# A kernel of two chained per-batch products: the result stores move from SyncE's queue to ScalarE's

## The chip, the cores and the metric

The kernel runs on one core of one Trainium2 chip. The metric is the device time of one execution in microseconds. Names of engines: PE is TensorE, DVE is VectorE, ACT is ScalarE, POOL is GpSimd, SP is SyncE, whose only work is to issue transfers and wait for them.

## The reference, cut to what matters

```
# x (128, 64, 512); itok_B_0_7, itok_B_1_198 (128,); weights (8, 64, 64) and (200, 64, 64)
w = L0_cond_weights[itok_B_0_7];   x = x + einsum('bct,bcd->bdt', x, w)
w = L1_cond_weights[itok_B_1_198]; x = x + einsum('bct,bcd->bdt', x, w)
```

Each of the 128 batches is a matrix of 64 channels by 512 time steps. It is multiplied by one of 8 matrices and added to itself, then the same with one of 200 matrices. x and the result are 16.8 MB each, in fp32.

## The kernel before

**What is computed.** For each batch the two steps are one 64x64 matrix, (W0 + 1)(W1 + 1). The kernel builds these matrices on the chip and multiplies each batch once.

**Tiles.** Four batches make a slot: 128 partitions by 1024 numbers, 0.5 MB. There are 32 slots (0 to 31), and two of them make a unit of 1 MB; there are 16 units (0 to 15). All of x stays in one SBUF tensor, `xy`, with a place of its own for each slot. The results are written over x there, and are stored from there. So no load waits for room, and no store frees any.

**The start.** SP loads the indices, unit 0 and slot 2. ACT loads the 8 first matrices and the other indices. POOL gathers the second matrices, one for each batch (2.1 MB, an indirect transfer on a queue of its own). PE turns the matrices (L175, L190; L180 is repeated work that keeps PE busy meanwhile), and DVE and ACT copy them (L248, L298). SP issues slot 3 and units 2 to 15 (L121) once DVE has copied the first 16 of the first matrices.

**The loop.** The 16 units are grouped in blocks: unit 0, unit 1, and then two units each (`BLOCKS`). `products` (L210) multiplies the two matrices of each batch of a block into PSUM. `copy_m` (L262) on DVE and ACT brings them to `m_diag`. `apply` (L229) multiplies the slots of a block, 8 matmuls for each slot as the trace counts them, into two of six PSUM banks, so three slots are in flight (`Y_RING` is 3): slot s waits for the copies of slot s - 3 on both engines. `copy_y` (L270) copies a slot's result from PSUM to `xy`; DVE takes one half of the batches' channels and ACT the other, two copies each for every slot.

**Order.** Nothing here is placed by a scheduler. PE's order is products(0), then for each block k products(k + 1) and apply(k). DVE and ACT run the same function `copies`: for each block the copies of its slots, then `copy_m` of block k + 2 (whose waits are L254 and L257). SP issues all loads and then all stores, on one queue. A store of unit v waits for both engines' copies of the unit's second slot; the last unit is stored as two slots:

```
            for v in range(UNITS - 1):
                store(2 * v, 2)
            store(SLOTS - 2, 1)
            store(SLOTS - 1, 1)
            for v in range(UNITS):
                sp.wait_ge(s_out[v], 32 if v == UNITS - 1 else 16)
```

`s_y_v` and `s_y_s` count the copies done on DVE and on ACT, two for each slot, and `s_out` the stores that have landed. `s_y_psum` counts the slots that PE has finished.

Of the kernel before, what the change touches and what calls it, by code (L numbers as in the profile page):

```python
# [5 lines left out]
def bass_cond_residual_kernel(  # L6
# [31 lines left out]
    SLOTS = B // SLOT  # L38
    UNIT = 2 * SLOT
    UNITS = B // UNIT  # L40
# [25 lines left out]
    out_view = out_dram.rearrange("(s b) (q i) t -> (b q) s (i t)", b=SLOT, i=J)  # L66

    ctx = ExitStack()
    with ctx:  # L69
        def sb(name, shape, dt):  # L70
            return ctx.enter_context(nc.sbuf_tensor(name, shape, dt))

        def sem(name):
            return ctx.enter_context(nc.semaphore(name))

        xy = sb("xy", [P, SLOTS, J * T], fp32)
# [34 lines left out]
        s_y_v = sem("s_y_v")  # L111
        s_y_s = sem("s_y_s")
        s_x = [sem(f"s_x{n}") for n in range(UNITS)]
        s_out = [sem(f"s_out{n}") for n in range(UNITS)]
# [3 lines left out]
        @block.sync  # L118
        def _(sp):
            def load(s, n):  # L120
                sp.dma_start(xy[:, s:s + n, :], x_view[:, s:s + n, :]).then_inc(s_x[s // 2], 16)  # L121

            sp.dma_start(cond[:, :], cond_dram.rearrange("(b o) -> b o", o=1)).then_inc(s_cond, 16)
            load(0, 2)
            load(2, 1)

            sp.wait_ge(s_w0b_early, EARLY * UNIT)
            load(3, 1)
            for v in range(2, UNITS):
                load(2 * v, 2)  # L130
            def store(s, n):

                sp.wait_ge(s_y_v, 2 * (s + n))
                sp.wait_ge(s_y_s, 2 * (s + n))
                sp.dma_start(out_view[:, s:s + n, :], xy[:, s:s + n, :]).then_inc(s_out[s // 2], 16)

            for v in range(UNITS - 1):
                store(2 * v, 2)
            store(SLOTS - 2, 1)
            store(SLOTS - 1, 1)  # L140
            for v in range(UNITS):
                sp.wait_ge(s_out[v], 32 if v == UNITS - 1 else 16)

        @block.gpsimd
        def _(pool):
            nc.gpsimd.memset(ident[:, :], 0.0).then_inc(s_zeros, 1)
            pool.wait_ge(s_zeros, 1)
            nc.gpsimd.affine_select(out=ident[:, :], in_=ident[:, :], compare_op=ALU.not_equal, fill=1.0,
                                    base=0, pattern=[[-1, P]], channel_multiplier=1).then_inc(s_ident, 1)

            pool.wait_ge(s_cond, 16)
            nc.gpsimd.indirect_dma_start(
                out=w1_rows[:, :, :].rearrange("b d e -> b (d e)"), out_offset=None,
                in_=w1_dram.rearrange("s d e -> s (d e)"),
                in_offset=bass.IndirectOffsetOnAxis(ap=cond[:, 0:1], axis=0)).then_inc(s_gather, 16)

            pool.wait_ge(s_subjects, 16)
            for first in range(EARLY * UNIT, B, 2 * UNIT):
                _, picked = nc.values_load_multi_w_load_instructions(  # L159
                    subjects[0:1, first:first + 2 * UNIT], engines=(POOL,), min_val=0, max_val=S0 - 1,  # L160
                    skip_runtime_bounds_check_because="subjects index the 8 matrices")
                if first == EARLY * UNIT:
                    pool.wait_ge(s_gather, 16)
                    pool.wait_ge(s_w0t, 4)
                for n in range(2 * UNIT):
                    v, odd, r = (first + n) // UNIT, n // SLOT % 2, n % SLOT
                    nc.gpsimd.tensor_copy(w0b[HALVES[odd], v * SLOT + r, :],  # L167
                                          w0t[HALVES[odd], bass.ds(picked[n] * C, C)]).then_inc(s_w0b, 1)
# [74 lines left out]
        def copy_w1(eng, copy, done, n):  # L243

            eng.wait_ge(s_w1_turned, n + 1)
            turned = psum[0:C, n % W1_RING, :].rearrange("q (k v o r) -> q o v r k", k=TURN, o=2, r=SLOT)
            for odd, rows in enumerate(HALVES):
                copy(w1[rows, :, n * TURN:(n + 1) * TURN].rearrange("q (v r) k -> q v r k", r=SLOT),  # L248
                     turned[:, odd, :, :, :]).then_inc(done, 1)

        def copy_m(eng, scale, done, odd, k):

            first, n = BLOCKS[k]
            eng.wait_ge(s_m_psum, k + 1)  # L254
            if first + n > M_RING:

                eng.wait_ge(s_y_psum, 2 * (first + n - M_RING))  # L257
            at = first % M_COLUMNS * J * C
            to = m_diag[:, odd, first % M_RING:first % M_RING + n, :, :].rearrange(
                "q v j (i b e) -> q b (v j) i e", i=J, b=2)  # L260
            for b in range(2):
                scale(to[:, b, :, :, :],  # L262
                      psum[:, M_BANKS[k] + odd, at:at + n * J * C].rearrange("q (w e i) -> q w i e", i=J, e=Q),
                      mask[:, b:b + 1]).then_inc(done, 1)

        def copy_y(eng, copy, done, i, s):

            eng.wait_ge(s_y_psum, s + 1)
            for h, rows in enumerate(HALVES):
                copy(xy[rows, s, i * T:(i + 1) * T], psum[HALVES[i], 2 * (s % Y_RING) + h, :]).then_inc(done, 1)  # L270

        def copies(eng, copy, scale, w1_done, m_done, y_done, odd):
            for n in range(odd, TURNS, 2):
                copy_w1(eng, copy, w1_done, n)
            eng.wait_ge(s_mask, 2 * SLOT)
            copy_m(eng, scale, m_done, odd, 0)
            copy_m(eng, scale, m_done, odd, 1)
            for k, (first, n) in enumerate(BLOCKS):
                for s in range(2 * first, 2 * (first + n)):
                    copy_y(eng, copy, y_done, odd, s)  # L280
                if k + 2 < len(BLOCKS):
                    copy_m(eng, scale, m_done, odd, k + 2)

        @block.vector
        def _(dve):
# [10 lines left out]
            for rows in HALVES:  # L296
                for j in range(J):
# [3 lines left out]
                        one[:, j, :, :, :].to_broadcast((C, S0, Q // J, J)), ALU.add).then_inc(s_w0t, 1)  # L301

            _, picked = nc.values_load_multi_w_load_instructions(
                subjects[0:1, 0:EARLY * UNIT], engines=(DVE,), min_val=0, max_val=S0 - 1,
                skip_runtime_bounds_check_because="subjects index the 8 matrices")
# [7 lines left out]
            diagonal = w1_rows[:, :, :].rearrange("b d e -> b (d e)")[:, ::C + 1]  # L313
            nc.vector.tensor_scalar_add(diagonal, diagonal, 1.0).then_inc(s_w1_plus, 1)  # L314
            copies(dve, nc.vector.tensor_copy, nc.vector.tensor_scalar_mul, s_w1_v, s_m_v, s_y_v, 0)

        @block.scalar
        def _(act):
            act.dma_start(w0_rows[:, :, :], w0_dram.rearrange("s (k j) d -> (s k) j d", j=ROWS)  # L319
                          ).then_inc(s_w0_rows, 16)  # L320
            act.dma_start(subjects[:, :], subject_dram.rearrange("(o b) -> o b", o=1)).then_inc(s_subjects, 16)

            act.wait_ge(s_w0_rows, 16)
            for n in range(TICKS):
                if n >= 1:
                    act.wait_ge(s_tick, n)
                nc.scalar.copy(w1[:, 0:ROWS, :], w0_rows[:, :, :]).then_inc(s_tick, 1)  # L327
            copies(act, nc.scalar.copy, nc.scalar.mul, s_w1_s, s_m_s, s_y_s, 1)


# [24 lines left out]
```

## Time and profile before

| | |
|---|---|
| median of 3 runs | 92.88 us (92.86 to 92.94) |
| the profiled execution | 92.97 us |
| its span, first to last instruction | 91.2 us |
| mean granted PE clock in the span | 0.976 |
| bytes moved | 35.93 MB, of them 16.8 MB loads of x and 16.8 MB stores |

The span is what the profile covers; 1.8 us of the profiled execution lie around it. A share of busy time is a share of the span. "Landing" of a transfer is the time from its issue until all of it has arrived and its semaphore says so. SP's waits and the time that an issue takes aren't counted as busy work. A queue is named by the profile: q1 is SP's, q10 is ACT's, q0 is POOL's.

### The profile page before, as it was taken

To read this page: it belongs to the slowest core of one execution; us is meant where nothing else is said; L and a number is where in the kernel's file an instruction comes from. 1 tells how busy PE (TensorE), PEld (TensorE's weight loads), DVE (VectorE), ACT (ScalarE), POOL (GpSimd) and SP (SyncE) were. 2 spreads that over 40 slices of the span, in tenths; PEclk is the share of its full clock that TensorE was granted. 3 is DMA by queue.
4 is the path that set the end of the run, shared out by engine and by line. 5 is a ranking of instruction groups with operands and counts; after the bars stand their busy time and mean duration, and the time that the engine had idled before them with its cause. 6 is when DMAs were issued, how large, how long until landed. Compare 5 with 4: busy or idle time off the path is not lost.

```text
span 91.2 us, 2427 instructions
## 1 busy us (share of the span) xinstructions
PE 79.2 (87%) x890; PEld 45.6 (50%) x890; DVE 61.8 (68%) x127; ACT 58.6 (64%) x117; POOL 23.4 (26%) x119
## 2 busy tenths in 40 slices
PE   0599979985999999999999999999999999999100
PEld 0488959974454544454454445445545444443000
DVE  1096009996287878787888787888778888788600
ACT  2899806886276776676777576777657676676500
POOL 3400039989999988000000000000000000000000
PEclk9999999999999999999999999999999999999955
DMA  0999999999999999999999999999999999999992
GB/s 12 335 438 422 453 361 420 411 406 415 406 408 408 406 408 413 415 394 417 408 403 415 420 419 420 410 424 415 419 415 419 415 422 422 419 419 404 417 404 104
DMA packets 9181, 35.93 MB, mean 394 GB/s; under 512 B 721, under 2 KB 850, under 8 KB 9042
## 3 DMA queue, kind: packets, MB, share of 16 engines
q1 hardware_dynamic: 8880, 33.56, 91.5%
q0 software_dynamic: 144, 2.10, 5.4%
q8 instruction: 7, 0.11, 0.5%
q10 hardware_dynamic: 146, 0.13, 0.5%
q14 instruction: 4, 0.03, 0.1%
HBM read 19.01 MB, written 16.78 MB: 392 GB/s over the span
## 4 chain that ended last, share of the span: by engine, by line
PE 70%; DMA 12%; DVE 9%; issue 1%; DVEq 1%; ACTq 0%; POOLq 0%
PE psum L229 62%; DMA w_rows<-in_L_cond_weights_dram,cond 10%; DVE w L248 7%; PE psum L210 7%; DMA subjects<-in_itok_B_dram 2%; DVEq L69 1%; DVE xy L270 1%; PE psum L190 1%; DVE m_diag L262 1%; ACTq L319 0%; DVE w_rows L314 0%; POOLq L159 0%; DVEq L254 0%
## 5 line engine op out<-in xcount | busy, mean ns | idle before, releaser
L229 PE MATMUL psum<-xy,m_diag 64*128 64x512 f32 x256 | 57.1, 595 | 0.5 <-DVE m_diag L262 0.5
L270 DVE COPY xy<-psum 64x512 f32<-64x512 f32 x64 | 43.7, 684 | 13.1 <-PE psum L229 12.1
L270 ACT COPY xy<-psum 64x512 f32<-64x512 f32 x64 | 37.2, 581 | 19.8 <-PE psum L229 19.0
L229 PEld LDWEIGHTS psum<-xy,m_diag 64*128 64x128 f32 x256 | 25.2, 187 | 26.7 <-issue 25.4
L167 POOL COPY w0b<-w0t 64x64 f32 x112 | 21.6, 235 | 10.1 <-DMA w_rows<-in_L_cond_weights_dram,cond 8.4
L210 PEld LDWEIGHTS psum<-w,w0b 64*32 64x32 f32 x512 | 5.6, 105 | 6.4 <-issue 3.8
L248 ACT COPY w<-psum 64x256 f32<-64x256 f32 x16 | 5.8, 364 | 4.0 <-PE psum L190 3.0
L180 PE MATMUL psum<-ident,w_rows 128*64 128x128 f32 x54 | 8.1, 326 | 0.0
L262 DVE TENSOR_SCALAR m_diag<-psum,mask 128x256 f32<-128x256 f32 (+1 forms) x18 | 7.2, 448 | 1.1 <-PE psum L210 0.9
L190 PE MATMUL psum<-ident,w_rows 128*64 128x128 f32 x64 | 7.2, 274 | 0.7 <-DVE w_rows L314 0.7
L327 ACT COPY w<-w_rows 128x256 f32<-128x256 f32 x18 | 7.3, 404 | 0.8 <-DMA w_rows<-in_L_cond_weights_dram 0.2
L180 PEld LDWEIGHTS psum<-ident,w_rows 128*64 128x64 f32 x54 | 7.3, 137 | 0.7
L210 PE MATMUL psum<-w,w0b 64*32 64x64 f32 x512 | 6.9, 224 | 0.9 <-DVE w L248 0.9
L262 ACT ACTIVATE m_diag<-psum,mask 128x256 f32<-128x256 f32 (+1 forms) x18 | 7.0, 447 | 0.9 <-PE psum L210 0.7
L248 DVE COPY w<-psum 64x256 f32<-64x256 f32 x16 | 6.7, 418 | 1.2 <-PE psum L190 0.8
L190 PEld LDWEIGHTS psum<-ident,w_rows 128*64 128x64 f32 x64 | 7.0, 151 | 0.9 <-DVE w_rows L314 0.9
L175 PE MATMUL psum<-ident,w_rows 128*64 128x128 f32 x4 | 1.0, 414 | 3.4 <-DMA w_rows<-in_L_cond_weights_dram 3.4
L298 DVE TENSOR_TENSOR w0t<-psum,ident 64x256 f32<-64x256 f32 x4 | 1.5, 412 | 3.3 <-PE psum L175 3.3
L314 DVE TENSOR_SCALAR w_rows<-w_rows 128x64 f32<-128x64 f32 x1 | 0.2, 224 | 4.2 <-DMA w_rows<-in_L_cond_weights_dram,cond 4.2
L327 ACT ACT_TABLE_LOAD x1 | 1.3, 1283 | 1.8 <-issue 1.8
L309 DVE COPY w0b<-w0t 64x64 f32 x16 | 2.1, 187 | 0.2
L175 PEld LDWEIGHTS psum<-ident,w_rows 128*64 128x64 f32 x4 | 0.5, 159 | 3.4 <-issue 3.4
(8 smaller groups left out, 2.3 us busy)
## 6 DMA issues: line engine op xcount, KB each, us to landing
xy<-in_x_dram SPq DMA_DIRECT2D x15, 1024.0 KB, 18.5
out_dram<-xy SPq DMA_DIRECT2D x15, 1024.0 KB, 14.8
xy<-in_x_dram SPq DMA_DIRECT2D x2, 512.0 KB, 5.9
out_dram<-xy SPq DMA_DIRECT2D x2, 512.0 KB, 4.7
w_rows<-in_L_cond_weights_dram ACTq DMA_DIRECT2D x1, 128.0 KB, 2.5
cond<-in_itok_B_dram SPq DMA_DIRECT2D x1, 0.5 KB, 2.3
subjects<-in_itok_B_dram ACTq DMA_DIRECT2D x1, 0.5 KB
w_rows<-in_L_cond_weights_dram,cond POOLq DMA_INDIRECT x1, 9.3
```

Of the source, the lines that this page charges most:

```text
L167: nc.gpsimd.tensor_copy(w0b[HALVES[odd], v * SLOT + r, :], w0t[HALVES[odd], bass.ds(picked[n] * C, C)]).then_inc(s_w0b, 1)
L175: last = nc.tensor.transpose(w0_psum[:, z * P:(z + 1) * P], w0_rows[:, z, :], ident[:, :])
L180: nc.tensor.transpose(psum[0:C, z, 0:P], w0_rows[:, z, :], ident[:, :])
L190: last = nc.tensor.transpose(psum[0:C, n % W1_RING, z * B:(z + 1) * B], w1_rows[:, :, n * TURN + z], ident[:, :])
L210: last = nc.tensor.matmul(psum[QUARTERS[r], M_BANKS[k] + odd, at:at + C], w0b[rows, v * SLOT + r, j * Q:(j + 1) * Q], w1[rows, v * SLOT + ...
L229: last = nc.tensor.matmul(psum[:, 2 * (s % Y_RING) + h, :], m_diag[rows, odd, v % M_RING, j, :], xy[rows, s, j * T:(j + 1) * T], start=j = ...
L248: copy(w1[rows, :, n * TURN:(n + 1) * TURN].rearrange("q (v r) k -> q v r k", r=SLOT), turned[:, odd, :, :, :]).then_inc(done, 1)
L262: scale(to[:, b, :, :, :], psum[:, M_BANKS[k] + odd, at:at + n * J * C].rearrange("q (w e i) -> q w i e", i=J, e=Q), mask[:, b:b + 1]).the ...
L270: copy(xy[rows, s, i * T:(i + 1) * T], psum[HALVES[i], 2 * (s % Y_RING) + h, :]).then_inc(done, 1)
L298: nc.vector.tensor_tensor(w0t[rows, :].rearrange("q (s j k y) -> q j s k y", s=S0, j=J, y=J)[:, j, :, :, :], turned[:, j, :, :, :], one[:, ...
L309: nc.vector.tensor_copy(w0b[HALVES[odd], v * SLOT + r, :], w0t[HALVES[odd], bass.ds(picked[n] * C, C)]).then_inc(s_w0b_early, 1)
L327: nc.scalar.copy(w1[:, 0:ROWS, :], w0_rows[:, :, :]).then_inc(s_tick, 1)
```

## The change

The stores leave SP. `store` becomes a function in the outer scope that issues on ACT's own queue, with the same two waits, now executed by ACT. In `copies`, ACT alone (`odd` is 1 there) calls it after the copies of each even slot s above 0, for the unit that ended with slot s - 1. The two stores of the last unit stand at the end of ACT's program. SP issues the loads and then waits for all stores, as before.

```
--- before
+++ after
@@ block.sync
             for v in range(2, UNITS):
                 load(2 * v, 2)
-            def store(s, n):
-
-                sp.wait_ge(s_y_v, 2 * (s + n))
-                sp.wait_ge(s_y_s, 2 * (s + n))
-                sp.dma_start(out_view[:, s:s + n, :], xy[:, s:s + n, :]).then_inc(s_out[s // 2], 16)
-
-            for v in range(UNITS - 1):
-                store(2 * v, 2)
-            store(SLOTS - 2, 1)
-            store(SLOTS - 1, 1)
             for v in range(UNITS):
                 sp.wait_ge(s_out[v], 32 if v == UNITS - 1 else 16)
@@ after copy_y
+        def store(s, n):
+
+            nc.scalar.wait_ge(s_y_v, 2 * (s + n))
+            nc.scalar.wait_ge(s_y_s, 2 * (s + n))
+            nc.scalar.dma_start(out_view[:, s:s + n, :], xy[:, s:s + n, :]).then_inc(s_out[s // 2], 16)
+
@@ copies
                 for s in range(2 * first, 2 * (first + n)):
                     copy_y(eng, copy, y_done, odd, s)
+                    if odd and s % 2 == 0 and s > 0:
+
+                        store(s - 2, 2)
@@ block.scalar
             copies(act, nc.scalar.copy, nc.scalar.mul, s_w1_s, s_m_s, s_y_s, 1)
+            store(SLOTS - 2, 1)
+            store(SLOTS - 1, 1)
```

The last rows of ACT's program before, slots 28 to 31. A row is an instruction with its line, and in brackets the semaphores that it waits for:

```order
L270 COPY xy<-psum 64x512 [waits s_y_psum]
L270 COPY xy<-psum 64x512
L270 COPY xy<-psum 64x512 [waits s_y_psum]
L270 COPY xy<-psum 64x512
L270 COPY xy<-psum 64x512 [waits s_y_psum]
L270 COPY xy<-psum 64x512
L270 COPY xy<-psum 64x512 [waits s_y_psum]
L270 COPY xy<-psum 64x512
L69 UNCONDITIONAL_BRANCH
```

And of the change, the same four slots (its line numbers are smaller by 10; L260 is L270 of before, L266 is the store):

```order
L260 COPY xy<-psum 64x512 [waits s_y_psum]
L260 COPY xy<-psum 64x512
L266 DMA out_dram<-xy 128x2x1024 [waits s_y_s,s_y_v]
L260 COPY xy<-psum 64x512 [waits s_y_psum]
L260 COPY xy<-psum 64x512
L260 COPY xy<-psum 64x512 [waits s_y_psum]
L260 COPY xy<-psum 64x512
L266 DMA out_dram<-xy 128x2x1024 [waits s_y_s,s_y_v]
L260 COPY xy<-psum 64x512 [waits s_y_psum]
L260 COPY xy<-psum 64x512
L266 DMA out_dram<-xy 128x1024 [waits s_y_s,s_y_v] x2
L69 UNCONDITIONAL_BRANCH
```

The stores of units 13 and 14 stand behind the copies of slots 28 and 30, and those of slots 30 and 31 behind all copies.

SP's program before, whose rows are the loads and then the stores:

```order
L123 DMA cond<-in_itok_B_1_198_dram 128x1
L121 DMA xy<-in_x_dram 128x2x1024
L121 DMA xy<-in_x_dram 128x1024
L121 DMA xy<-in_x_dram 128x1024 [waits s_w0b_early]
L121 DMA xy<-in_x_dram 128x2x1024 x14
L135 DMA out_0_dram<-xy 128x2x1024 [waits s_y_s,s_y_v] x15
L135 DMA out_0_dram<-xy 128x1024 [waits s_y_s,s_y_v] x2
```

In the changed kernel the two rows of L135 are gone from SP, and the five above them stay as they are. The order on PE, DVE and POOL is the same in both kernels.

## Rows read from the trace of the kernel before

**Rows 1.** The page's part 2: busy tenths in 40 slices of the span
```profile
PE   0599979985999999999999999999999999999100
...
DMA  0999999999999999999999999999999999999992
```

**Rows 2.** The chain that ended last: start us, us, what; from 22.44 us on
```profile
22.44 3.70 PE psum L229 x16
...
39.21 7.07 PE psum L229 x32
...
70.70 13.96 PE psum L229 x64
84.66 0.02 issue
84.68 0.68 DVE xy L270
85.36 0.72 DVEq L69
```

**Rows 3.** Busy time by stretch, with PEclk, DMA share and GB/s at the end
```profile
7.00:14.00 7.00, 6.35 (x51) 5.87 (x50) 1.95 (x14) 3.81 (x10) 1.09 (x6) 1.00 0.97 402
28.00:35.00 7.00, 7.00 (x94) 3.32 (x94) 5.47 (x10) 4.56 (x9) 6.45 (x35) 1.00 1.02 405
35.00:42.00 7.00, 7.00 (x94) 3.32 (x94) 5.77 (x10) 5.12 (x10) 1.10 (x6) 1.00 1.03 409
49.00:56.00 7.00, 7.00 (x94) 3.38 (x94) 5.86 (x9) 5.25 (x10) 0.00 (x0) 1.00 1.03 420
77.00:84.00 7.00, 7.00 (x34) 3.10 (x32) 5.60 (x9) 4.78 (x9) 0.00 (x0) 1.00 1.02 416
84.00:91.00 7.00, 0.63 (x4) 0.00 (x0) 1.73 (x3) 1.31 (x3) 0.00 (x0) 0.71 0.79 321
```

**Rows 4.** DMA queues of the whole span: packets, MB, share of 16 engines
```profile
q1 hardware_dynamic: 8880, 33.56, 91.5%
```

**Rows 5.** SP's last load issue (L121, duration in ns, landing in us), and its first store
```profile
L121 SPq DMA_DIRECT2D xy<-in_x_dram x1: 5425/5425/5425, 29.7 to 29.7; - x1
...
DMA to landing us min/median/max: 21.0/21.0/21.0
...
35.20 2.27 SPq L135 DMA_DIRECT2D out_dram<-xy  x1
```

**Rows 6.** Timeline of ACT: its copies of slot 2 and of slot 5
```profile
28.90 0.58 ACT L270 COPY xy<-psum 64x512 f32<-64x512 f32 x1 [0.67 <-PE psum L229]
...
35.04 1.19 ACT L270 COPY xy<-psum 64x512 f32<-64x512 f32 x2 [0.53 <-PE psum L229]
```

**Rows 7.** The last three stores (L135), and the timeline from 82 us on
```profile
L135 SPq DMA_DIRECT2D out_dram<-xy x3: 345/345/372, 82.7 to 86.1; - x3
...
DMA to landing us min/median/max: 4.6/4.7/5.6
...
82.67 3.78 SPq L135 DMA_DIRECT2D out_dram<-xy  x3
...
82.97 1.19 ACT L270 COPY xy<-psum 64x512 f32<-64x512 f32 x2 [0.53 <-PE psum L229]
...
84.68 1.40 DVE L270 COPY xy<-psum 64x512 f32<-64x512 f32 x2 [0.32 <-PE psum L229]
```

**Rows 8.** The first issues of ACT and SP, and the landing of ACT's first
```profile
0.75 0.41 ACTq L319 DMA_DIRECT2D w_rows<-in_L_cond_weights_dram  x1
1.18 0.54 ACTq L321 DMA_DIRECT2D subjects<-in_itok_B_dram  x1
...
0.75 0.38 SPq L123 DMA_DIRECT2D cond<-in_itok_B_dram  x1
...
w_rows<-in_L_cond_weights_dram ACTq DMA_DIRECT2D x1, 128.0 KB, 2.5
```

**Rows 9.** The wait of L257 near 46.3 us, and ACT's timeline there
```profile
L257 ACTq EVENT_SEMAPHORE  x1: 17/17/17, 46.3 to 46.3; - x1
...
46.33 1.19 ACT L270 COPY xy<-psum 64x512 f32<-64x512 f32 x2 [0.53 <-PE psum L229]
```

**Rows 10.** ACT's longest wait: us in total, times, longest
```profile
ACT xy L270 <- PE psum L229: 19.0, 32, 1.6
```

**Rows 11.** DMA queues from 10 to 12 us, the gather (q0) beside the loads
```profile
q0 software_dynamic: 49, 0.56, 65.4%
q1 hardware_dynamic: 31, 0.13, 17.8%
```

## The prediction

> **What bounds the kernel now.** I read four views in this order: busy shares, the chain of waits, the transfers by stretch, the single stores at the end.
>
> The page's head [rows 1] shows two resources full at once: PE at 9 tenths nearly everywhere, and the 16 DMA engines at 9 in 38 of 40 slices, moving some 410 GB/s. The chain of waits [rows 2] runs from 22.44 us on through PE alone (32 slots, with short pieces of L210 between) to 84.66 us, then through DVE's last two copies. So PE sets when the last result exists. But the DMA engines are not waiting for it: in the stretches [rows 3] they move 405 to 409 GB/s while only loads are in flight (28 to 49 us), 416 to 420 while only stores are (56 to 84 us), and 321 on average in the last stretch, where the work runs out. All 33.56 MB of x and result lie on SP's one queue, q1, in issue order [rows 4]: the last load is issued at 29.7 us and lands 21.0 us later, at 50.7; the first store therefore moves nothing before 50.7, though SP issues it at 35.2 [rows 5] and slot 2, the one after its own two, is already copied from 28.9 on [rows 6].
>
> Is the end set by PE or by the queue? Two stores answer [rows 7]. The 1 MB store of unit 14 takes 5.6 us from issue to landing, the 0.5 MB store of slot 31 4.6 us. Unloaded, 128 KB took 2.5 us [rows 8], of which 0.13 MB / 410 GB/s = 0.3 is transfer: 2.2 us fixed (estimate, from a load). The two would then need 2.2 + 2.6 = 4.8 and 2.2 + 1.3 = 3.5 us. So 0.8 to 1.1 us of each is queueing behind older bytes. The bound at the end is the **transfer total**, with PE only about 1 us behind it.
>
> **The change, part by part.**
>
> *Bytes and instructions.* The same 17 stores of the same shapes; 17 issues leave SP and go to ACT. No copy, matmul or load is changed. The only thing that can move the end is when stores reach the DMA engines and how fast these work with two queues in flight.
>
> *ACT's time.* 17 issues x 0.372 us (the issue of an unblocked store [rows 7]; ACT's own took 0.406 and 0.542 [rows 8]) = 6.3 to 9.2 us on ACT's sequencer. Does it delay copies? The wait of L257 stands behind the two copies of a slot in ACT's program, and it is recorded at 46.3 us, when the copies have just begun (46.33 to 47.52) [rows 9]. So the sequencer runs ahead of the engine, and an issue runs beside the copies in front of it. A slot lasts 1.72 us (82.97 to 84.68 [rows 7]), its two copies 1.19: 0.54 us at most, begun with the copies, ends before they do. ACT also waited 19.0 us for PE in 32 waits [rows 10]. Cost: 0.
>
> *The added waits.* The stores' waits now stand in ACT's stream, and the copies of the next slot are queued behind them. For unit v they ask for both engines' copies of slot 2v+1, and they are reached when slot 2v+2 is done on PE. DVE's two copies take 1.40 us [rows 7], less than a slot of 1.72, so the wait is already met. Only the last two stores are different: nothing is queued behind them. Cost: 0.
>
> *How late the stores come.* Unit 14: SP issued it at 82.67, now it follows slot 30's copies, whose release is at 82.97: 0.3 us later (not 1.7, since the sequencer runs ahead). Slot 30: from 84.4 to about 84.7, after slot 31's copies are dispatched. Slot 31: waits for DVE's copy, which ends at 86.08, as before. The queueing of 0.8 us on unit 14 covers the 0.3. Cost: 0; without that cover it would be 0.3.
>
> *How early they come.* Store 0 can go at 28.9 us, when slot 2's copies begin [rows 6], and need not wait behind the loads of its queue until 50.7. From about 30 us both kinds share the engines. Loads that have not landed at 30: 20.7 us x 0.407 = 8.4 MB, units 8 to 15. At half of 412 GB/s, 206, they last until 70.8 us. PE starts unit 15 at 82.97 - 1.72 = 81.2. So loads stay 10 us ahead, PE keeps its pace, and the bytes are only reordered. Work is conserved: gain 0.
>
> Is half right? The nearest row with two queues in flight is the gather beside the loads: from 10 to 12 us 49 packets on q0 and 31 on q1 [rows 11], so neither queue starves the other. The loads need 8.4 MB in 51 us, 164 GB/s, 40% of 412.
>
> *Rate with both directions mixed.* Nothing in this trace shows it: loads and stores never overlap. The bounds are the nearest stretches: all at 405 or all at 420 [rows 3] over the 41 us of mixing. At 405 instead of 412, 41 x 1.7% = 0.7 us later; at 420, 0.8 us earlier. Below 405 lies only the 402 of the stretch with gather and loads on two queues, and it also holds SP's wait. I take 412, the middle: it is what the same bytes get now. The early end is capped: 2.1 MB remain to be issued from 83.0 on, so the last landing is at 83.0 + 2.2 + 5.1 = 90.3 against 90.7 now (86.1 + 4.6), 0.4 us; and since the 2.2 is an estimate from a load, I let the range go to 0.7.
>
> [...]
>
> **Sum:** 0 + 0 + 0 + 0 on the profiled execution's 92.97 us; its span of 91.2 and the 1.8 around it stay. The median of the three runs is 92.88, 0.09 below, so I forecast **92.9 us**. A change under 0.2% (0.19 us) can't be told from none here.
>
> **The cases.**
>
> 1. *Conserved work*, 92.9 us: chance 0.37. For it: DMA full in every slice [rows 1], same bytes.
>
> 2. *Mixing is faster*, or spreads better: 420 or more while both directions run; the queue empties early and the cap of 0.4 us applies, 92.5 (to 92.2 if the fixed part of a store is less than 2.2). For it: stores alone run at 418. Against: engines are already at a share of 1.02, with no gap to fill. Chance 0.27.
>
> 3. *Mixing is slower.* This is the case on the other side: reads and writes of HBM alternate on the same 16 engines from 30 to 71 us, and each packet takes some per cent longer. At 400 GB/s, 3% of 41 us = 1.2 us: 94.1 us. Every per cent costs 0.4; it decides from half a per cent on, since no cover lies behind it. For it: the two pure stretches already differ by 2.5%, so direction matters. Against: no row shows alternation. Chance 0.20.
>
> 4. *ACT is held at an issue.* SP's last load issue lasts 5.4 us, from 29.7 to 35.1 [rows 5]: its queue is full. If an ACT issue has to wait for that, copies wait too. Worst: store 0, from 28.9 to 35.1 + 0.4. Slot 3's copies (1.19) then end at 36.7, while PE wants their PSUM banks for slot 6 as soon as slot 5 is done, at 35.04 [rows 6]: 1.7 us lost on PE, less the queueing left at the end (0.8 - 0.3): 1.2, 94.1 us. If only store 1 (about 33.3) is held, to 37.7, slot 5's copies end at 38.9, before PE begins slot 8 at 39.21 [rows 2], and nothing is lost. Against it: ACT's and SP's first issues, 0.41 and 0.38 us, both began at 0.75 [rows 8], and overlapped. Chance 0.11. [...]
>
> 5. *Loads starve*: they get under 40%. PE waits for x late; the last load lands near 85, then two slots (3.4), copies (1.4) and the last store (4.6) follow: span 95, some 96.5 us. Against: the even packets of [rows 11]. Chance 0.05.
>
> **From cases to numbers.** Faster 0.27 (case 2), same 0.37 (case 1), slower 0.36 (cases 3 to 5). Range 92.2 to 94.4: from the low end of case 2 to case 3 at 3.5% and case 4 in full; left out are case 5 and the tails of 2 and 3, together 0.15 or so. Case 1's own range is 92.7 to 93.1.
>
> **What the profile after must show.** Stores on q10 from 29 us, about 17 MB on each of q1 and q10; SP's last load landing near 71; 16 DMA engines full at 412; ACT's issues at 0.4 to 0.55 us, PE without idle time from 22.4 to 84.7; unit 14's store issued at 83.0, slot 31's at 86.1. The rate in the stretches from 35 to 70 decides between cases 1, 2 and 3: 405 or below is case 3, 418 or above case 2. An ACT issue longer than 1 us while SP still issues is case 4; PE idle before L229 with a load as releaser is case 5. I am wrong in substance if the stretches stay at 412 and the time still moves by over 0.3 us.

## The result, and the profile after

| | before | after |
|---|---|---|
| median of 22 runs | 93.00 us | 92.73 us |
| the profiled execution | 92.97 us | 92.78 us |
| its span | 91.2 us | 91.0 us |

The ratio of after to before is 0.9964, with a 95% interval of 0.9952 to 0.9975: the change makes the kernel 0.36% faster, 0.33 us of 93.0. That is small, but clear of no change. The ratio leaves out three executions (one before, two after) that took 2% longer or more, so it isn't exactly the quotient of the medians. The forecast of 92.9 us was "no change", so its sign was missed, although 92.73 lies within the range of 92.2 to 94.4. It lies between case 2 (92.5) and case 1 (92.9), and still within case 1's own range of 92.7 to 93.1.

The head of the page after, to be read against [rows 1]. Its columns are 40 slices of the span.

```profile
PE   0499939994999999999999999999999999999200
...
DMA  0999989999999999999999999999999999999993
GB/s 9 334 411 421 461 342 427 412 412 407 411 411 402 412 400 414 409 421 420 418 418 414 423 420 418 416 418 421 423 407 423 418 418 421 421 414 376 414 420 140
```

Both resources are as full as before. The DMA engines carry something in every slice; what has moved is how much. One slice near the end stands out, 376.

The queues of the whole span, after (packets, MB, share of 16 engines):

```profile
q1 hardware_dynamic: 4512, 16.78, 46.3%
q10 hardware_dynamic: 4514, 16.91, 45.8%
```

The same bytes as in [rows 4], now on two queues. From 34 to 64 us of the changed kernel the two read:

```profile
q10 hardware_dynamic: 1616, 6.23, 51.0%
q1 hardware_dynamic: 1618, 6.23, 50.8%
```

Half each, to within two packets, as the prediction had assumed. (A packet is one record of a DMA engine in the trace; from 34 to 49 us 1484 of the 1579 packets before have 4096 bytes, and of the others 93 have 4.)

Now the stretches. Of the kernel before (in [rows 3] the borders are others), with GB/s as the last number:

```profile
34.00:49.00 15.00, 15.00 (x192) 7.18 (x190) 12.01 (x20) 10.32 (x19) 2.04 (x11) 1.00 1.02 407
49.00:62.00 13.00, 13.00 (x127) 6.14 (x128) 10.45 (x16) 8.97 (x16) 0.00 (x0) 1.00 1.03 419
...
82.00:84.00 2.00, 2.00 (x12) 0.86 (x10) 1.65 (x3) 1.45 (x3) 0.00 (x0) 1.00 1.00 406
```

And of the changed one:

```profile
34.00:49.00 15.00, 15.00 (x190) 7.04 (x188) 12.18 (x20) 10.47 (x20) 2.91 (x16) 1.00 1.03 416
49.00:62.00 13.00, 13.00 (x122) 5.86 (x118) 10.43 (x16) 8.97 (x16) 0.00 (x0) 1.00 1.03 419
...
82.00:84.00 2.00, 2.00 (x12) 0.97 (x10) 1.62 (x4) 1.42 (x4) 0.00 (x0) 1.00 0.95 385
```

This is where the time came from. Before, 34 to 49 us carried loads alone, at 407 GB/s; after, loads and stores together, at 416. From 49 us on there is no difference, 419 in both, though before these are stores alone (from 50.7 us) and after they are mixed. So the mixed rate of 416 to 419 isn't the middle of 407 and 419: it is near that of stores. (416 - 407) x 15 us = 0.135 MB, which take 0.32 us at 419. From 82 to 84 us the changed kernel gives 0.04 MB back, 0.1 us; the share of the engines falls from 1.00 to 0.95 there.

The ratio is worth 0.33 us, so the size fits. It is no closed account: the two traced executions differ by 0.19 us only, and the changed one had moved 0.11 MB less by 33 us (12.48 against 12.59), before its stores had a share. The rates themselves repeat. From 34 to 49 us, eleven traced executions read 415 or 416 GB/s: the changed kernel twice, and the nine versions below that keep stores among the loads. The kernel before and its version without one store both read 407.

The packets show what is faster. Counted in the two traces from 34 to 49 us, the 1484 packets of 4096 bytes before take 163.5 ns in the mean, and 37% of them take 159; the 1513 after take 160.3 ns, and 96% take 159. That is 2.0% less time for a packet and 2.0% more packets: the gain is in how long packets take, not in gaps between them, of which the share of the engines, 1.02 before and 1.03 after, shows none.

The end of the changed kernel, its timeline from 83 us on (start, us, engine, line; L266 is the store, L260 the copy):

```profile
83.16 0.58 ACT L260 COPY xy<-psum 64x512 f32<-64x512 f32 x1 [0.53 <-PE psum L219]
...
83.22 0.38 ACTq L266 DMA_DIRECT2D out_dram<-xy  x1
...
84.88 0.58 ACT L260 COPY xy<-psum 64x512 f32<-64x512 f32 x1 [0.53 <-PE psum L219]
...
84.94 0.36 ACTq L266 DMA_DIRECT2D out_dram<-xy  x1
...
86.31 0.35 ACTq L266 DMA_DIRECT2D out_dram<-xy  x1
```

The store of unit 14 is issued at 83.22 us, 0.06 us after the first of slot 30's two copies begins (83.16), while they run: ACT's sequencer is ahead of its engine here, as [rows 9] had suggested. SP had issued it 0.30 us ahead of them [rows 7]. The last store waits for DVE's copy in both. The last three stores land in 4.2 to 4.8 us, where they took 4.6 to 5.6 before [rows 7]: the queue at the end is shorter.

And the start of the sharing, ACT's first two stores and SP's last load issues in the changed kernel:

```profile
29.14 0.42 ACTq L266 DMA_DIRECT2D out_dram<-xy  x1
33.57 0.40 ACTq L266 DMA_DIRECT2D out_dram<-xy  x1
...
L121 SPq DMA_DIRECT2D xy<-in_x_dram x1: 10435/10435/10435, 29.9 to 29.9; - x1
DMA to landing us min/median/max: 37.8/37.8/37.8
```

SP's last issue lasts 10.4 us where it lasted 5.4 before [rows 5], and from 33 us on its queue gets half of the packets. ACT's second store is issued in the middle of it, at 33.57 us, and takes 0.40 us. ACT isn't held. The last load lands at 29.9 + 37.8 = 67.7 us, 13.7 us ahead of PE's need, and PE's only waits are those of the start, as before.

### The profile page after: what moved, and what is told of

Same layout as the page of the kernel before. It is cut to its first block, busy times and chain, and to the rows that moved or that the text cites. A ratio compares the mean times of both kernels' runs of the same rounds, so it can differ in the third digit from the quotient of the medians.

```text
span 91.0 us, 2427 instructions
## 1 busy us (share of the span) xinstructions
PE 78.5 (86%) x890; PEld 44.7 (49%) x890; DVE 61.8 (68%) x127; ACT 58.6 (64%) x117; POOL 23.4 (26%) x119
## 3 DMA queue, kind: packets, MB, share of 16 engines
q1 hardware_dynamic: 4512, 16.78, 46.3%
## 4 chain that ended last, share of the span: by engine, by line
PE 70%; DMA 13%; DVE 9%; issue 1%; DVEq 1%; ACTq 0%; POOLq 0%
PE psum L219 62%; DMA w_rows<-in_L_cond_weights_dram,cond 10%; DVE w L238 7%; PE psum L200 7%; DMA subjects<-in_itok_B_dram 2%; DVEq L69 1%; DVE xy L260 1%; PE psum L180 1%; DVE m_diag L252 1%; ACTq L318 0%; DVE w_rows L313 0%; POOLq L149 0%; DVEq L244 0%
## 5 line engine op out<-in xcount | busy, mean ns | idle before, releaser
L260 DVE COPY xy<-psum 64x512 f32<-64x512 f32 x64 | 43.7, 683 | 13.2 <-PE psum L219 12.2
L260 ACT COPY xy<-psum 64x512 f32<-64x512 f32 x64 | 37.2, 581 | 19.8 <-PE psum L219 19.0
L180 PE MATMUL psum<-ident,w_rows 128*64 128x128 f32 x64 | 7.2, 274 | 1.4 <-DVE w_rows L313 1.4
L180 PEld LDWEIGHTS psum<-ident,w_rows 128*64 128x64 f32 x64 | 7.0, 152 | 1.6 <-DVE w_rows L313 1.6
L170 PE MATMUL psum<-ident,w_rows 128*64 128x128 f32 x54 | 7.5, 308 | 0.0
L170 PEld LDWEIGHTS psum<-ident,w_rows 128*64 128x64 f32 x54 | 6.7, 128 | 0.7
L165 PE MATMUL psum<-ident,w_rows 128*64 128x128 f32 x4 | 1.0, 415 | 3.5 <-DMA w_rows<-in_L_cond_weights_dram 3.5
L165 PEld LDWEIGHTS psum<-ident,w_rows 128*64 128x64 f32 x4 | 0.5, 158 | 3.5 <-issue 3.5
```

The costliest lines, as they stand in the source:

```text
L165: last = nc.tensor.transpose(w0_psum[:, z * P:(z + 1) * P], w0_rows[:, z, :], ident[:, :])
L170: nc.tensor.transpose(psum[0:C, z, 0:P], w0_rows[:, z, :], ident[:, :])
L180: last = nc.tensor.transpose(psum[0:C, n % W1_RING, z * B:(z + 1) * B], w1_rows[:, :, n * TURN + z], ident[:, :])
```

## The experiments

Two theories at first. **A**: loads and stores in flight together move faster than loads alone, and that is the gain. **B**: the gain comes from ACT's queue, or from SP being free. Each run's expectation stands as it was written before it. A ratio is to the kernel before, on the same chip, with its 95% interval.

**One queue, mixed.** The kernel before, with five loads and stores in turn:

```
+            for v in range(2, 11):
+                load(2 * v, 2)
             for v in range(UNITS - 1):
                 store(2 * v, 2)
+                if 11 + v < UNITS:
+                    load(2 * (11 + v), 2)
```

> The kernel before, with all transfers on SP's one queue, but the last five loads stand in turn with the first five stores (store 0, load 11, store 1, load 12, ...). Theory A in its wide form (what counts is that both directions are in flight, from whichever queue): the engines see 1 MB of one kind and then 1 MB of the other, and as each engine works through them on its own only the borders overlap; the stretch 34 to 49 is 411 to 417 GB/s and the ratio 0.997 to 1.000. Theory A in its narrow form (two queues, so that each engine alternates packet by packet): 409 while loads pass, 418 while stores do, and a ratio of 1.000 +- 0.001. Rival B: 1.000 as well.

Measured: 92.71 us, ratio 0.9964 (0.9947 to 0.9980), the very ratio of the change. The ratio is just below the 0.997 that the wide form of A had as its low end. Its stretches:

```profile
34.00:49.00 15.00, 15.00 (x192) 7.12 (x190) 12.10 (x20) 10.39 (x19) 2.15 (x12) 1.00 1.03 415
49.00:62.00 13.00, 13.00 (x122) 6.19 (x118) 10.45 (x16) 8.97 (x16) 0.00 (x0) 1.00 1.03 419
```

415 on SP's queue alone. The run also holds both kinds in one execution: store 0 lands at 40.5 us, and the packets take 163.9 ns in the mean from 34 to 37.5 us, loads alone, and 159.8 from 38 to 49, with stores among them. B falls: neither ACT nor a second queue is needed. So does A in its narrow form.

**Loads on two queues, unmixed.** ACT issues loads 12 to 15 at slots 2 to 5; SP's stores start behind all loads:

```
-            for v in range(2, UNITS):
+            for v in range(2, 12):
                 load(2 * v, 2)
+            sp.wait_ge(s_x[14], 16)
@@ copies
+                    if odd and 2 <= s < 6:
+                        v = 10 + s
+                        nc.scalar.dma_start(xy[:, 2 * v:2 * v + 2, :], x_view[:, 2 * v:2 * v + 2, :]).then_inc(s_x[v], 16)
```

> Two queues without mixing of directions: SP loads units 2 to 11, ACT issues loads 12 to 15 at slots 2 to 5, and SP issues the stores only once load 14 has landed, so that they stand behind the last loads. From 34 to 46 us both queues carry loads. Theory A' (loads alone are slow, on one queue or two): 34 to 46 us at 406 to 411 GB/s, ratio 0.999 to 1.002. Rival (two queues in flight make the engines faster, whatever they carry): 415 to 418 there, ratio 0.996 to 0.998.

Measured: 95.32 us, 1.0227 (1.0206 to 1.0249). For the question of the queues the rate counts, not the time:

```profile
34.00:46.00 12.00, 12.00 (x118) 5.45 (x114) 9.76 (x16) 8.51 (x16) 2.31 (x12) 1.00 1.03 408
...
64.00:82.00 18.00, 18.00 (x146) 8.73 (x144) 14.23 (x23) 12.11 (x22) 0.00 (x0) 1.00 1.02 405
```

Two queues of loads (676 packets on q10, 584 on q1) give 408, what one gives in the kernel before from 34 to 46 us (408): the second queue of loads added nothing. The time was missed by 2 us, and the second row tells why. The stores from 64 to 82 us move at 405, not at 418 [rows 3]. The wait on load 14 had let the engines run short at 47 to 52 us (354 and 361 GB/s in two slices of its page).

**Stores late on ACT's queue.** The changed kernel, first store behind slot 12, then two for each even slot until caught up:

```
-                    if odd and s % 2 == 0 and s > 0:
-                        store(s - 2, 2)
+                    if odd and s % 2 == 0 and s >= 12:
+                        u = s // 2 - 1
+                        for v in ([2 * (u - 5), 2 * (u - 5) + 1] if u < 10 else [u]):
+                            store(2 * v, 2)
```

> The stores stay on ACT's queue, but the first is issued behind slot 12 (about 49 us), when the loads have nearly all landed; two units for each even slot until it has caught up at slot 20. So two queues, next to no mixing. Theory A (loads and stores in flight together move at about 417 GB/s, loads alone at 409): the stretch from 34 to 49 us is back at 407 to 410 GB/s and the time is that of the kernel before, ratio 0.999 to 1.001. Rival B (the gain comes from ACT's queue or from a free SP, not from mixing): the ratio stays at 0.996 to 0.997, as in the changed kernel.

Measured: 95.91 us, 1.0318 (1.0279 to 1.0356). Neither theory gave that. The page has 289 and 308 GB/s at 47 to 52 us, since the first stores came after the loads had run out, and then 404 from 64 to 82 us. As a test of A against B the run says nothing; as a sign of something else it is the same as the one above.

**An idle stretch on purpose.** Was it the idle stretch that slowed the stores behind it? The kernel before, with one wait:

```
+            sp.wait_ge(s_x[UNITS - 1], 16)
             for v in range(UNITS - 1):
                 store(2 * v, 2)
```

> The kernel before with SP waiting for the last load to land before it issues the first store, so that all 16 engines are idle together for some 1 to 2 us at 51 us; then stores alone, back to back. Theory A': 54 to 82 us at 416 to 420 GB/s as before; the time grows by the gap alone, less what was in hand: 94.2 to 95.0 us. Rival F: stores behind the gap move at 403 to 408 GB/s, 3% of 38 us = 1.1 us more: 95.3 to 96.3 us.

Measured: 97.69 us, 1.0488 (1.0443 to 1.0532), beyond both ranges: the engines were short of work from 48 to 54 us, 1.3 MB less than before or 3.1 us, where I had expected 1 to 2 us.

```profile
50.00:52.00 2.00, 2.00 (x13) 0.82 (x12) 1.65 (x3) 1.42 (x4) 0.00 (x0) 1.00 0.09 35
54.00:64.00 10.00, 10.00 (x168) 4.87 (x166) 8.14 (x13) 7.05 (x14) 0.00 (x0) 1.00 1.02 397
64.00:82.00 18.00, 18.00 (x146) 8.20 (x146) 14.31 (x24) 12.20 (x23) 0.00 (x0) 1.00 1.02 403
82.00:84.00 2.00, 2.00 (x12) 0.96 (x10) 1.65 (x3) 1.45 (x3) 0.00 (x0) 1.00 1.02 410
```

The engines stand still together at 50 to 52 us, and the same stores, back to back on the same queue, then move at 397 to 403 GB/s, and slowly better, instead of 418. Their packets take 167.6 ns in the mean from 54 to 64 us and 165.3 from 64 to 82, where those of the kernel before take 160. So the rate isn't a matter of the kind of bytes alone. This called for a third theory, **F**: the rate is a state that the engines keep, lower from a common start.

**Loads alone behind three stores**, twice. If F is right, loads behind stores are fast. All on SP's queue:

```
-            for v in range(2, UNITS):
+            for v in range(2, 10):
                 load(2 * v, 2)
+            for v in range(3):
+                store(2 * v, 2)
+            for v in range(10, UNITS):
+                load(2 * v, 2)
-            for v in range(UNITS - 1):
+            for v in range(3, UNITS - 1):
                 store(2 * v, 2)
```

> The kernel before, all on SP's queue, with stores 0, 1 and 2 put between load 9 and load 10. So from about 43 to 57 us the engines carry loads alone, but behind a stretch of stores. Theory A' (the kind of bytes sets the rate: loads alone 409 GB/s, anything with stores in it 417): 44 to 56 us is at 407 to 410, and the time lies between before and the changed kernel, ratio 0.998 to 1.000, since only the borders are faster. Rival F (the rate is a state that the engines keep: 409 from a common start after an idle stretch, 417 once a change of kind has set them apart): 44 to 56 us is at 415 to 419 although only loads move, and the ratio is 0.996 to 0.997, as with five loads and stores in turn.

Measured: 93.27 us, 1.0027 (1.0004 to 1.0050), with 411 from 44 to 56 us. The third store waited for PE while little was queued, and the page shows 373 and 403 near 39 to 43 us. The second version puts the three stores behind load 11 and not behind load 9 (`range(2, 12)` and `range(12, UNITS)`), so that the queue can't run dry:

> As the run with loads behind three stores, but the stores stand behind load 11, with two more loads queued ahead of them, so that the queue can't run dry at 39 us. Loads alone from about 49 to 57 us. Theory A' (kind of bytes): 40 to 47 us (stores alone) at 416 to 420, 50 to 56 us (loads alone) at 407 to 411; total ratio 0.999 to 1.0005, since each byte moves at the rate of its kind. Rival F (a state kept from before): 50 to 56 us at 415 to 419, and the ratio 0.996 to 0.998.

Measured: 93.08 us, 0.9984 (0.9971 to 0.9998), between the two ranges.

```profile
40.00:47.00 7.00, 7.00 (x73) 3.14 (x73) 5.52 (x10) 4.66 (x10) 0.00 (x0) 1.00 1.03 421
50.00:56.00 6.00, 6.00 (x90) 2.99 (x88) 4.88 (x9) 4.31 (x8) 0.00 (x0) 1.00 1.03 415
```

Loads alone move at 415 here and at 411 in the first version, where loads alone from the start have 407. The means hide what happens inside. Here loads alone have 419 GB/s from 50 to 53 us, with 88% of the packets at 159 ns, and 411 from 53 to 56, with 33%. In the first version they have 414 from 44 to 50 us and 409 from 50 to 56, where 25% take 159 ns, fewer than the 37% of the kernel before. So loads alone behind stores keep the high rate for some 5 us and then lose it. F is right in that the past counts, and wrong for loads in that the state lasts; after those 5 us loads alone are slow in both runs, at 411 and 409 GB/s.

**An idle stretch ahead of the mixing.** Is mixing immune to it? The changed kernel with

```
             for v in range(2, UNITS):
+                if v == 6:
+                    sp.wait_ge(s_x[5], 16)
                 load(2 * v, 2)
```

> The changed kernel, but SP issues load 6 only when load 5 has landed, so that all engines are idle together for about 1 us at 25 to 26 us, ahead of the mixing. Mixing theory (packets of both directions in turn are what keeps the engines at 417): 35 to 62 us at 415 to 419 all the same, and the time grows by the gap, 0.8 to 1.6 us: 93.5 to 94.4. History theory (a common restart costs rate until the engines have drifted apart): 35 to 50 us at 400 to 410, and the time 94.5 or more.

Measured: 97.32 us, 1.0440 (1.0413 to 1.0467).

```profile
24.00:28.00 4.00, 4.00 (x80) 2.05 (x78) 3.20 (x6) 3.01 (x6) 3.71 (x21) 1.00 0.42 109
28.00:34.00 6.00, 6.00 (x90) 2.85 (x88) 4.75 (x10) 4.06 (x9) 5.39 (x30) 1.00 0.93 307
34.00:49.00 15.00, 15.00 (x192) 7.11 (x190) 12.00 (x20) 10.30 (x20) 2.08 (x12) 1.00 1.02 416
...
64.00:82.00 18.00, 18.00 (x146) 8.67 (x144) 14.21 (x23) 12.10 (x23) 0.00 (x0) 1.00 1.03 419
```

The time is beyond the mixing theory's 94.4, for the gap was larger than meant: from 12 to 28 us this run moved 315 GB/s against 409 in the changed kernel, and from 28 to 34 us 307 against 404, together 2.1 MB or 5.0 us less, enough for the whole loss of 4.3 us (97.3 - 93.0). The rates are those of the mixing theory: mixed traffic behind the gap moves at 416, and at 419 from 64 us on, part of it stores alone. So mixing reached the high rate behind an idle stretch, where stores alone stayed at 397 to 403. The two runs aren't quite alike: here 6 us of uneven loads lie between the idle stretch and the first stores.

**One slot later.** How much later may the last stores come before the time grows, in other words what is in hand at the end? The changed kernel with `if odd and s % 2 == 1 and s > 2: store(s - 3, 2)`:

> The changed kernel with every store but the last two one slot (1.72 us) later: unit 14 at 84.9 us with slot 30's store right behind it. Theory C: the queue has about 0.8 us of work left when unit 14 is issued in the changed kernel, so a shift of 1.7 us costs what exceeds that, 0.6 to 1.2 us, ratio to before 1.003 to 1.009; the engines are partly idle from 83.5 to 86. Rival D': the last engine has 1.5 us or more in hand: less than 0.3 us, ratio below 1.000.

Measured: 93.77 us, 1.0077 (1.0049 to 1.0104), 1.1% or 1.05 us above the change. 82 to 84 us is at 322 GB/s and 84 to 86 at 229. A shift of 1.72 us costs 1.05, so some 0.7 us were in hand, as theory C expected.

**The last slots singly.** The changed kernel storing slots 28, 29 and 30 one by one (`if odd and s > SLOTS - 4: store(s - 1, 1)`), and the same on SP's queue with five loads and stores in turn:

> The changed kernel, with slots 28, 29, 30 stored one by one, each behind the next slot's copies, so that the first half of unit 14 is issued at 81.4 us instead of 83.2. Theory C (the gain of the change is cut at the end, because the DMA engines run dry at 83 to 84 us: 385 GB/s there): the dip goes away, 82 to 84 us at 410 or more, and the time is 0.1 to 0.2 us below that of the changed kernel, ratio to before 0.994 to 0.996. Rival D (the dip belongs to engines that would have ended early anyway; the last engine to finish sets the time): dip gone, same time as the changed kernel, 0.996 to 0.9975.

> All transfers on SP's queue with five loads and stores in turn (ratio 0.9964 when run alone), and slots 28 and 29 stored one by one as well, so that half of unit 14 is issued 1.7 us sooner. If the last release still holds up the last engine, the time falls by a further 0.1 to 0.3 us: ratio 0.993 to 0.9955. If the 0.6 us of queue that the changed kernel has left at its end covers the release, nothing is gained: 0.9955 to 0.9975.

Measured: 92.84 us, 0.9984 (0.9966 to 1.0003), and 92.89 us, 0.9970 (0.9948 to 0.9992). Nothing is gained in either; the first ratio is even above theory D's range, which its interval reaches. Theory C, that the end cuts the gain of the change, falls; D stands: what is still queued covers the release.

**Four loads outstanding.** The changed kernel with `if v >= 6: sp.wait_ge(s_x[v - 4], 16)` ahead of each load:

> The changed kernel, but SP issues load v only when load v - 4 has landed, so its queue is never full. In the changed kernel store 0 was issued at 29.1 us, its bytes moved from 32.8 on, and it landed 10.4 us after its issue. Theory H (ACT's transfer waits its turn behind the load that SP's full queue holds back, though ACT itself does not): now store 0 lands some 5 to 6 us after its issue and mixing starts at about 30 us; SP's issues stay below 0.6 us. The time gains 3 us x 2% = 0.06 us, not measurable: ratio to before 0.995 to 0.997. Rival: the 4 us are a start-up cost of ACT's queue, and store 0 still takes 9 us or more.

Measured: 92.77 us, 0.9977 (0.9956 to 0.9998), an interval that covers the expected 0.995 to 0.997 in part.

```profile
29.34 0.42 ACTq L268 DMA_DIRECT2D out_dram<-xy  x1
...
L268 ACTq DMA_DIRECT2D out_dram<-xy x1: 417/417/417, 29.3 to 29.3; - x1
DMA to landing us min/median/max: 9.8/9.8/9.8
L121 SPq DMA_DIRECT2D xy<-in_x_dram x9: 367/368/368, 19.5 to 48.4; - x9
```

From 19.5 us on SP's issues are all 0.37 us, so its queue is never full, and store 0 still takes 9.8 us. Theory H falls: what holds the first bytes of the second queue back isn't SP's full queue. The rival, a start-up cost of ACT's queue, falls too: in the run with late stores ACT's first store was issued at 49.5 us, when next to no loads were left, and landed 4.3 us later.

**One store left out**, four times, to find the floor that PE sets, the earliest end that its last result allows. In the changed kernel; in the kernel before; in the changed one with the last slots singly; and on one queue, mixed:

> The changed kernel leaving out the store of unit 6 (1 MB, 2.5 us of all engines), so that part of the result isn't written. It measures how far PE's end is behind the transfers' end. Theory C' (PE, through the release of the last stores, is 0.7 us behind the last engine): the time falls by 0.6 to 1.2 us and not by 2.5, to 91.5 to 92.1; the engines are partly idle from 82 us on. Rival (transfers are the only bound): 90.2.

> The kernel before, leaving out the store of unit 6 (1 MB, 2.5 us of all engines), so that part of the result isn't written. With PE's end as the floor, it can only fall to the floor that the changed kernel showed with the same store left out (92.4 profiled, median 92.7, ratio 0.9947): theory: ratio 0.990 to 0.995, a gain of 0.5 to 0.9 us out of 2.5, and the same time as there within 0.3 us. Rival (before is bound by transfers far beyond PE): 90.5 us, 0.973.

> The changed kernel with slots 28 to 30 stored singly, leaving out the store of unit 6 (that part of the result isn't written). Theory G (with transfers out of the way, the end is the release of the last 2 MB plus their transfer, about 6.5 us behind unit 14's issue; storing slot 28 1.7 us earlier lowers it until the last slot's own release, 3.2 us behind its issue, is the floor): 0.4 to 0.9 us below the changed kernel with unit 14 stored whole (0.9947): ratio 0.986 to 0.991. Rival: the floor is ACT's end itself, and the ratio stays at 0.993 to 0.996.

> All transfers on SP's queue, five loads and stores in turn, leaving out the store of unit 6 (not written). Theory G: SP issues unit 14 0.35 us earlier against PE than ACT does, so the floor is that of the kernel before without this store: ratio 0.985 to 0.990. Rival (mixing itself costs something at the end): 0.993 to 0.996, as in the changed kernel.

The edit is the same in all: the store of unit 6 and SP's wait for it are gone. "Release" is when ACT's copies of slot 31 begin, from the timeline of each profiled execution.

| kernel, without the store of unit 6 | ratio | release, us | span, us | from release to end |
|---|---|---|---|---|
| changed | 0.9947 (0.9915 to 0.9979) | 85.11 | 90.6 | 5.5 |
| before | 0.9873 (0.9834 to 0.9913) | 84.57 | 89.6 | 5.0 |
| changed, last slots singly | 0.9908 (0.9881 to 0.9935) | 84.71 | 90.1 | 5.4 |
| one queue, mixed | 0.9908 (0.9876 to 0.9940) | 84.74 | 89.8 | 5.1 |
| *all stores:* before | 1 | 84.68 | 91.2 | 6.5 |
| *all stores:* changed | 0.9964 | 84.88 | 91.0 | 6.1 |

Of 2.5 us of transfer taken away, the kernel before gives back 1.2 us and the changed one 0.2 by the ratios; the latter isn't told from none, and is less than the 0.6 to 1.2 that I expected. By single traces, transfers are the bound by about 1.5 us before (6.5 - 5.0) and by 0.6 after (6.1 - 5.5). The difference of 0.9 has two parts. 0.4 is the shorter way from release to end with all stores (6.5 - 6.1); half of it is the shorter span, and half the later release of that execution. 0.5 is a higher floor (5.5 against 5.0), of which unit 14's issue, 0.36 us later against PE, could be the larger part: both kernels with SP's stores have the low floor, 5.0 and 5.1. My expectation that before and changed would meet within 0.3 us was wrong by this. Theory G's ratio was met in the third row, and just missed in the fourth (0.9908 against 0.985 to 0.990, inside the interval). But the third row's trace shows a floor lower by 0.1 us only, so what makes the floor isn't settled. The release itself differs by 0.5 us between these executions: the gather lands between 12.6 and 13.1 us, in the order of the releases, and from slot 0's release to slot 31's it is 60.2 us in each.

**The changed kernel again**, beside the last three:

> The changed kernel once more, beside the next three on one chip. Every theory: ratio to before 0.995 to 0.998.

Measured: 92.76 us, 0.9977 (0.9952 to 1.0002), with 416 GB/s from 34 to 49 us. The medians agree with the first series (92.73); this interval alone would not tell the change from none.

No version that writes the whole result beats the changed kernel beyond its interval; one queue with five loads and stores in turn equals it.

## Why the prediction was wrong, point by point

- **The bound.** Right. Transfers set the end and PE is close behind. The queueing of 0.8 to 1.1 us that I read from two stores was measured at 1.2 (ratio) to 1.5 (trace) by leaving a store out.
- **The cost on ACT.** Right. An issue takes 0.35 to 0.42 us, beside the copies, and PE waits for nothing new.
- **Unit 14's store 0.3 us later, at no cost.** Right: 0.06 behind the copies instead of 0.30 ahead, 0.36 in all. The cover was there, and it shrank from about 1.5 us to 0.6; one queue mixed, where SP issues unit 14 early, has the same time (0.9964).
- **The half share.** Right, 1616 packets against 1618. Sharing began at 33 us and not at 30, as the last section shows, so the last load landed at 67.7 instead of 70.8.
- **"I take 412, the middle: it is what the same bytes get now."** This is the step that failed, and the only one. The mixed stretch runs at 416 to 419. That is 0.32 us gained in the stretch that had held loads alone, against the 0 of my sum, and as much as the whole result. I had treated a direction as something that each byte carries with it. With the other end of my own bounds, 420, the sum would have given the 0.4 us of case 2. Loads alone over 21 us at 407 and stores at 418 were in my rows; what I lacked was a reason to expect either end, and I took the middle for a conservative choice. Against case 2 I had held that the engines, at a share of 1.02, had no gap to fill; the gain needed none, since the packets became shorter (160.3 ns against 163.5). By the time alone 92.73 also fits case 1's own range; it is the rate, 417 from 34 to 67 us where case 2's sign was 418, that speaks for case 2.
- **Case 2's cap of 0.4 us.** Its reason, that the last 2 MB are released late, was not what held the gain. Storing the last slots singly gained nothing, and the gain is of the size of the rate's own 0.32. The cap is near, though: by the traces without unit 6 the floor begins about 0.6 us further.
- **Case 3, mixing slower.** It has the right place, the rate with both directions in flight, and the wrong sign.
- **Case 4, ACT held at an issue.** It did not happen. ACT issued a store in 0.40 us inside SP's issue of 10.4 us. The two issues of [rows 8] that spoke against the case were both short (0.41 and 0.38 us); here one of the two is long, and the other is still not held.

## What to carry to other kernels

When the DMA engines are full, read the GB/s of loads alone, of stores alone and of both together as three numbers (here 407, 419 and 416 to 419), and don't take the third for the mean of the first two. Here letting stores into the load phase was worth 2% of that phase, and the issuing engine was worth nothing: one queue with five loads and stores in turn had the same ratio, 0.9964. Before moving an issue behind work at the end of a kernel, find what is in hand there by leaving a transfer out; 0.36 us was free here, 1.7 us cost 1.05.

## What the runs showed of the hardware that I had not expected

- **Three kinds of traffic, three behaviours of the packets.** Of the packets of 4096 bytes, 96% take 159 ns in the changed kernel from 34 to 49 us, when both directions run (416 to 419 GB/s). In stretches of loads alone 25 to 57% of them do, with a mean of 163.2 to 163.9 ns (405 to 411 GB/s), and behind stores too, once some 5 us have passed. Stores alone kept what they found: 96% and 419 GB/s behind loads without a break (the kernel before, 64 to 82 us), a third of the packets and 401 to 404 GB/s from 54 to 82 us behind a stretch in which the engines were idle or short of work (the kernel with the idle stretch, with late stores, and with loads on two queues).
- **A common pause cost more than its length.** That follows for stores alone in the same three kernels, which had 401 to 404 GB/s up to 82 us, some 30 us behind it, and 408 to 410 from 82 to 88; mixed traffic behind a pause ran at 416. No run shows why.
- **The second queue started late beside a busy one.** ACT's first store was issued at 29.14 us and landed 10.4 us later, of which its 1.05 MB take 5 us at half of 416 GB/s, an estimate. With SP's queue never full it still took 9.8 us, and a load of the same size on ACT's queue, in the run with loads on two queues, 10.6. With next to nothing left on SP's queue a store took 4.3. From 31 to 33 us, the queue view of the changed kernel has 11 packets of q10 against 194 of q1, and from 33 to 35 us 103 against 106:

```profile
q1 hardware_dynamic: 194, 0.75, 98.3%
q10 hardware_dynamic: 11, 0.05, 5.5%
...
q10 hardware_dynamic: 103, 0.42, 51.9%
q1 hardware_dynamic: 106, 0.39, 48.4%
```

- **SP's full queue held only SP.** SP stood in one issue for 10.4 us while ACT's, issued at 33.57 us inside it, took 0.40 us. That outstanding loads make SP's issues long shows where SP keeps at most four of them out: its nine issues from 19.5 us on take 0.37 us each.
